# Part of the inverse roots and of the final sums of a recurrent block with experts moves to other engines, with new call orders

## What is computed

```python
xn = _layernorm(x)
s = attn_ref(xn)       # layer norm, k, v, r from mixes of a token and the one before it,
                       # running exp-weighted sums over time (wkv), output product, + xn;
                       # then layer norm, square(relu(xk @ f_kw)) @ f_vw, times sigmoid(xr @ f_rw), + x
shared_out = _swiglu(xn, shared_gate, shared_up, shared_down)
top_id = argmax(xn @ gate_w.T); score = sigmoid(max(xn @ gate_w.T))
routed_out = sum over e of _swiglu(where(top_id == e, xn * score, 0), w_gate[e], w_up[e], w_down[e])
out = x + s * silu(shared_out + routed_out)
```

## Time and profile before

| | |
|---|---|
| time, median of 3 runs | 515.05 us (514.98 to 516.02) |
| time of the profiled execution | 514.26 us |
| span of its instructions | 512.5 us |
| PE busy | 453.8 us (89%) |
| DVE busy | 394.2 us (77%) |
| ACT busy | 338.9 us (66%) |
| POOL busy | 327.3 us (64%) |

### The profile page before, as it was taken

How to read it: one execution, slowest core, us unless ns; L and a number is a source line. 1 busy time by engine, 2 the same in 40 slices (tenths; PEclk the granted TensorE clock), 3 DMA queues, 4 the chain that set the end, 5 groups by cost and what they waited for, 6 DMA issues and landing times. The chain is left out here.

```text
span 512.5 us, 9573 instructions
## 1 busy us (share of the span) xinstructions
PE 453.8 (89%) x2689; PEld 339.8 (66%) x2689; DVE 394.2 (77%) x896; ACT 338.9 (66%) x661; POOL 327.3 (64%) x347
## 2 busy tenths in 40 slices
PE   0879897869499898999899989998999998999995
PEld 0656665537257686978697969786978564555663
DVE  4698987889386879688959895889588999677362
ACT  2687766535185769676968686769686859395634
POOL 6437888788785368878787868678857544434010
PEclk9978899969889999999999989999999999999998
DMA  8213641111621045655555546555644346874200
GB/s 249 83 51 91 227 146 42 44 37 60 191 74 44 17 135 165 191 162 161 167 177 159 164 139 195 160 162 165 178 149 139 104 59 110 140 103 63 42 22 20
DMA packets 55060, 61.33 MB, mean 120 GB/s; under 512 B 5904, under 2 KB 43153, under 8 KB 54944
## 3 DMA queue, kind: packets, MB, share of 16 engines
q1 hardware_dynamic: 42672, 47.11, 31.6%
q0 software_dynamic: 11184, 11.94, 10.9%
q10 hardware_dynamic: 1152, 1.67, 1.0%
HBM read 46.97 MB, written 17.59 MB: 126 GB/s over the span
## 5 line engine op out<-in xcount | busy, mean ns | idle before, releaser
L1624 POOL DMA_INDIRECT routed_out<-xh,xs x71 | 77.4, 1090 | 44.1 <-ACT xh L1042 26.9
L475 PEld LDWEIGHTS bank_ring<-xh,ew 128*128 128x128 f32 x568 | 73.0, 194 | 19.2 <-issue 18.5
L1612 POOL DMA_INDIRECT tokens_by_expert<-xn,pos x64 | 71.4, 1116 | 19.5 <-issue 19.5
L475 PE MATMUL bank_ring<-xh,ew 128*128 128x128 f32 x568 | 75.8, 277 | 0.0
L419 PEld LDWEIGHTS bank_out<-fvw,kk 128*128 128x128 f32 x512 | 63.4, 192 | 12.3 <-issue 8.5
L419 PE MATMUL bank_out<-fvw,kk 128*128 128x128 f32 x512 | 66.4, 275 | 0.0
L1619 POOL TENSOR_SCALAR xs<-xs 128x128 f32<-128x128 f32 x71 | 57.2, 809 | 7.7 <-DMA xs<-tokens_by_expert 5.8
L1032 ACT ACTIVATE px<-bank_ring 128x256 f32<-128x256 f32 x71 | 27.2, 383 | 38.1 <-PE bank_ring L475 37.5
L2170 DVE TENSOR_TENSOR hx<-px,bank_ring 128x256 f32<-128x256 f32 x71 | 29.1, 409 | 25.4 <-ACT px L1032 19.2
L984 ACT ACTIVATE z<-x,x_sm 128x128 f32<-128x128 f32 x64 | 26.3, 482 | 27.8 <-POOL x_sm L1597 27.6
L489 PE MATMUL bank_ring<-ew,hx 128*128 128x128 f32 x284 | 43.4, 275 | 0.2 <-issue 0.2
(11 more groups left out here) (177 smaller groups left out, 1106.8 us busy)
## 6 DMA issues: line engine op xcount, KB each, us to landing
ew<-ex_w SPq DMA_DIRECT2D x71, 384.0 KB
xi<-x SPq DMA_DIRECT2D x19, 256.0 KB, 3.7
xs<-tokens_by_expert SPq DMA_DIRECT2D x71, 66.0 KB, 2.7
ew<-routed_out SPq DMA_DIRECT2D x16, 256.0 KB, 3.1
out<-x SPq DMA_DIRECT2D x2, 1664.0 KB
out<-xn POOLq DMA_DIRECT2D x13, 256.0 KB, 4.8
routed_out<-xh,xs POOLq DMA_INDIRECT x71, 2.8
tokens_by_expert<-xn,pos POOLq DMA_INDIRECT x64
```

Of the source, the lines that this page charges most:

```text
L475: last = nc.tensor.matmul(part(GU[n % 2], q, P), part(w, q, P), xt[:, 0:P], start=True, stop=True)
L1612: nc.gpsimd.indirect_dma_start(xs_dram, bass.IndirectOffsetOnAxis(ap=POS[:, t:t + 1], axis=0), XN[:, t * XROW:(t + 1) * XROW], None).then_ ...
L1624: nc.gpsimd.indirect_dma_start(routed_dram, bass.IndirectOffsetOnAxis(ap=XS[(n - 2) % NXS][:, CH:CH + 1].bitcast(i32), axis=0), XH[n % NXH ...
```

## The change

Five things change. **Roots:** `first(c)` takes 4 columns. DVE makes the second layer norm's variance in three parts (chunk 0, chunks 1 to 3, chunks 4 to 15: `second_variance`), whose inverse roots come from POOL for chunk 0 and from ACT's Ln and Exp for the others (`second_rstd`). Of `rstd_of_x2` only the power stays on POOL; DVE does the additions around it (`make_x2`, `bias_of_x2`). **Moved tiles:** `make_d1` and `make_rw` of chunks 0 to 3 go from POOL to DVE. **Final sums:** those of chunks 0 to 10 become one addition each on DVE, in place in the shared result. **Weights:** ACT issues the load of the shared expert's upper weights before the attention's, and four semaphores take the place of one. **Call orders:** every engine's list except SP's is written in another order; 64 scatters count on 8 semaphores where they had 16. The core of the diff:

```diff
+R2_PARTS = (0, 1, 4, CHUNKS)
+ON_VECTOR = (0, 1, 2, 3, 4, 5, 6, 7, 8, 9, 10)
...
+        def summed(p):
+            before = sum(1 for m in SUMS[:p] if m in ON_VECTOR)
+            return (s_fd, before + 1) if SUMS[p] in ON_VECTOR else (s_fy, p - before + 1)
 
...
             logits(0)
             first_transpose(1)
-            pe.wait_ge(s_wa, 16 * 5)
-            shared_part(0, 0)
+            shared_part(0, 1)
             logits(1)
             first_transpose(2)
...
-                                (ATT[:, :], att_w, s_wa), (SUP[:, :], sh_up, s_wa), (SDN[:, :], sh_dn, s_wa),
-                                (FKW[:, :], f_kw, s_wa), (FVW[:, :], f_vw, s_wa)):
+                                (SUP[:, :], sh_up, s_wu), (ATT[:, :], att_w, s_wa), (SDN[:, :], sh_dn, s_wd),
+                                (FKW[:, :], f_kw, s_wf), (FVW[:, :], f_vw, s_wf)):
                 act.dma_start(dst, src).then_inc(s, 16)
...
@@ -939,8 +935,15 @@
                 act.wait_ge(s_rt, g * PLACE + 1)
                 nc.scalar.activation(part(SC, g, GT), part(MX, g, GT), ACT.Tanh, scale=0.5).then_inc(s_th, 1)
 
+            def second_rstd(k):
+                a, b = R2_PARTS[k] * TPC, R2_PARTS[k + 1] * TPC
+                act.wait_ge(s_v2, 3 * k + 3)
+                nc.scalar.activation(R2[:, a:b], V2[:, a:b], ACT.Ln).then_inc(s_r2, 1)
+                act.wait_ge(s_r2, 2 * k + 1)
+                nc.scalar.activation(R2[:, a:b], R2[:, a:b], ACT.Exp, scale=-0.5).then_inc(s_r2, 1)
+
             def halve_output_weights():
-                act.wait_ge(s_wa, 16 * 5)
+                act.wait_ge(s_wa, 16)
                 nc.scalar.activation(part(ATT, 3, CH), part(ATT, 3, CH), ACT.Copy, scale=0.5).then_inc(s_half, 1)
 
...
             def final_part(m):
-                act.wait_ge(s_fy, SUMS.index(m) + 1)
-                nc.scalar.activation(part(XT, m, CHUNK), RING[2][:, :], ACT.Silu).then_inc(s_fw, 1)
+                act.wait_ge(*summed(SUMS.index(m)))
+                y = part(XT, m, CHUNK) if m in ON_VECTOR else RING[2][:, :]
+                nc.scalar.activation(part(XT, m, CHUNK), y, ACT.Silu).then_inc(s_fw, 1)
 
             nc.scalar.preload_act_table_set("natural_log_exp_and_others")
...
             def first(c):
-                a, b = 2 * c * TPC, 2 * (c + 1) * TPC
-                pool.wait_ge(s_ve, 2 * (c + 1))
-                nc.gpsimd.tensor_tensor(RS[:, a:b], VE[:, a:b], NH[:, 0:2 * TPC], ALU.pow).then_inc(s_rs, 1)
+                pool.wait_ge(s_ve, c + 1)
+                nc.gpsimd.tensor_tensor(part(RS, c, TPC), part(VE, c, TPC), NH[:, 0:TPC], ALU.pow).then_inc(s_rs, 1)
 
             def make_d1(c):
                 pool.wait_ge(s_h1, c + 1)
@@ -1582,20 +1589,14 @@
                     pool.wait_ge(s_mix, 3 * c)
                 nc.gpsimd.tensor_tensor(batches(D1[:, :]), now(H1), before(H1), ALU.subtract).then_inc(s_d1, 1)
 
+            def second_rstd_of_first():
+                b = R2_PARTS[1] * TPC
+                pool.wait_ge(s_v2, 3)
+                nc.gpsimd.tensor_tensor(R2[:, 0:b], V2[:, 0:b], NH[:, 0:b], ALU.pow).then_inc(s_r2, 2)
+
             def rstd_of_x2(c):
-                mean, var = stats(MV2, 0, TPC)
-                pool.wait_ge(s_mv2, TPC * (c + 1))
-                if c > 0:
-                    pool.wait_ge(s_z2, TPC * c)
-                settle(pool)
-                nc.gpsimd.tensor_scalar(SM2[:, 0:TPC], var, EPS, None, ALU.add).then_inc(s_sm2, 1)
-                nc.gpsimd.tensor_scalar(SM2[:, 2 * TPC:3 * TPC], mean, -1.0, None, ALU.mult).then_inc(s_nm2, 1)
                 pool.wait_ge(s_sm2, c + 1)
                 nc.gpsimd.tensor_tensor(SM2[:, TPC:2 * TPC], SM2[:, 0:TPC], NH[:, 0:TPC], ALU.pow).then_inc(s_rs2, 1)
-                pool.wait_ge(s_nm2, c + 1)
-                pool.wait_ge(s_rs2, c + 1)
-                nc.gpsimd.tensor_tensor(SM2[:, 2 * TPC:3 * TPC], SM2[:, 2 * TPC:3 * TPC], SM2[:, TPC:2 * TPC],
-                                        ALU.mult).then_inc(s_nb2, 1)
...
-                a = 2 * c * TPC
                 dve.wait_ge(s_mv, TPC * c + TPC)
-                nc.vector.tensor_scalar(VE[:, a:a + TPC], var, EPS, None, ALU.add).then_inc(s_ve, 1)
-                nc.vector.tensor_scalar(VE[:, a + TPC:a + 2 * TPC], var, 1.0 + EPS, EPS * EPS, ALU.mult, ALU.add)\
-                  .then_inc(s_ve, 1)
+                nc.vector.tensor_scalar(part(VE, c, TPC), var, EPS, None, ALU.add).then_inc(s_ve, 1)
 
             def first_bias(c):
-                a, b, t = c * TPC, (c + 1) * TPC, 2 * c * TPC
+                a, b = c * TPC, (c + 1) * TPC
                 mean, var = stats(MV, a, b)
                 dve.wait_ge(s_rs, c + 1)
-                nc.vector.scalar_tensor_tensor(NB[:, a:b], mean, -1.0, RS[:, t:t + TPC], ALU.mult, ALU.mult)\
+                nc.vector.scalar_tensor_tensor(NB[:, a:b], mean, -1.0, RS[:, a:b], ALU.mult, ALU.mult)\
                   .then_inc(s_nb, 1)
-                nc.vector.tensor_tensor(R2[:, a:b], VE[:, t:t + TPC], RS[:, t:t + TPC], ALU.mult).then_inc(s_v2, 1)
-                dve.wait_ge(s_v2, c + 1)
-                nc.vector.tensor_tensor(R2[:, a:b], R2[:, a:b], RS[:, t + TPC:t + 2 * TPC], ALU.mult).then_inc(s_r2, 1)
+
+            def second_variance(k):
+                a, b = R2_PARTS[k] * TPC, R2_PARTS[k + 1] * TPC
+                mean, var = stats(MV, a, b)
+                dve.wait_ge(s_mv, R2_PARTS[k + 1] * TPC)
+                dve.wait_ge(s_rs, R2_PARTS[k + 1])
+                nc.vector.tensor_tensor(V2[:, a:b], var, RS[:, a:b], ALU.mult).then_inc(s_v2, 1)
+                dve.wait_ge(s_v2, 3 * k + 1)
+                nc.vector.tensor_tensor(V2[:, a:b], V2[:, a:b], RS[:, a:b], ALU.mult).then_inc(s_v2, 1)
+                dve.wait_ge(s_v2, 3 * k + 2)
+                nc.vector.tensor_scalar(V2[:, a:b], V2[:, a:b], EPS, None, ALU.add).then_inc(s_v2, 1)
...
                     nc.vector.bn_aggr(part(MV2, j, 2), part(BS2, j, 6)).then_inc(s_mv2, 1)
+                mean, var = stats(MV2, 0, TPC)
+                dve.wait_ge(s_mv2, TPC * c + TPC)
+                nc.vector.tensor_scalar(SM2[:, 0:TPC], var, EPS, None, ALU.add).then_inc(s_sm2, 1)
+
+            def bias_of_x2(c):
+                mean, var = stats(MV2, 0, TPC)
+                dve.wait_ge(s_rs2, c + 1)
+                nc.vector.scalar_tensor_tensor(SM2[:, 2 * TPC:3 * TPC], mean, -1.0, SM2[:, TPC:2 * TPC],
+                                               ALU.mult, ALU.mult).then_inc(s_nb2, 1)
+
+            def make_d1(c):
+                dve.wait_ge(s_h1, c + 1)
+                if c > 0:
+                    dve.wait_ge(s_mix, 3 * c)
+                nc.vector.tensor_tensor(batches(D1[:, :]), now(H1), before(H1), ALU.subtract).then_inc(s_d1, 1)
+
+            def make_rw(c):
+                dve.wait_ge(s_tn, c + 1)
+                dve.wait_ge(s_iq, c + 1)
+                if c > 0:
+                    dve.wait_ge(s_att, c)
+                nc.vector.tensor_tensor(RW[:, :], NUM, LQ[:, :], ALU.mult).then_inc(s_rw, 1)
 
...
+
+            def final_sum(m):
+                p = SUMS.index(m)
+                dve.wait_ge(s_fr_in[p % 4], 16 * (p // 4 + 1))
+                dve.wait_ge(s_sh, m + 1)
+                nc.vector.tensor_tensor(part(XT, m, CHUNK), part(XT, m, CHUNK), RR[p % 4], ALU.add).then_inc(s_fd, 1)
 
```

More of the change, by code:

```diff
@@ L585, in _ @@
+            shared_part(9, 0)
+            key(3)
+            value(3)
+            shared_part(9, 1)
             ffn_receptance(0)
+            pe.wait_ge(s_wf, 16 * 2)
             ffn_key(0, 0)
@@ L828, in _ @@
-            z2_transpose(11)
-            expert_slot(71)
-            value(13)
-            expert_slot(72)
-            late_part(11, 0)
+            ffn_key(10, 1)
+            expert_slot(56)
+            ffn_key(10, 2)
+            ffn_key(10, 3)
+            expert_slot(57)
+            attention_out(11)
+            ffn_value(10, 0)
+            expert_slot(58)
+            receptance(13)
+            expert_slot(59)
+            key(13)
+            ffn_value(10, 1)
+            expert_slot(60)
```

1755 lines of the change are left out of this document (884 added, 871 removed).

## The result

The changed kernel takes 479.6 us (median of 4 runs, 476.0 to 483.3) where the kernel before took 515.2 in the same comparison: a ratio of 0.928, 95% interval 0.923 to 0.934. The profiled run, 483.25 us, is the slowest of the four, 1.5% above the fastest, and the ratio is of the three others (476.0 to 479.9). Measured again beside the first experiments it took 478.5 us (6 runs, 477.9 to 480.8), ratio 0.930 [0.927, 0.933]. The forecast was 491, range 478 to 506.

A forecast was written before the change was run, and what follows sets the result against it. TensorE's list was taken as the bound behind slot 0, with waits deciding the front. Front 160, slots 245.9, tail 78.3 and the last 5.8 gave a span of 490.0 us, plus 1.76 makes 491.8, stated as 491, range 478 to 506.

The forecast's parts named there:

- Final sums: Tail: 22 products of 0.86 us, 18.9 us, leave TensorE; VectorE gets 7.6 us; about 14 us gained after the new wait.
- The shift into the slots: One more chunk's work before slot 72: 15.5 us longer in the slots, 15.6 shorter in the tail, neutral at unchanged fill.
- The new wait of 6 us at chunk 13: Tail: TensorE stands 6 us at chunk 13's receptance for VectorE's mixes, bounds 0 and 10; tail 78.3 us.
- Front, 9 us: Before slot 0: GpSimd loses 13.5 us, last scatter at 143, slot 0 at 160, 9 us earlier; bounds 152 and 169.
- Slots, 245.9: Slot stretch: 227.5 us of TensorE work at fill 0.925, VectorE 83% busy; bounds 240.7 and 252.8.
- Weights and ScalarE's roots, 0: Shared weights' load with four semaphores, and ScalarE's extra table loads and activations in the front: 0 us.
- (1): Rival: VectorE sets the slots' pace, 255 us, time 501; chance 0.22 together with (2) and the rule's case.
- (3): Rival: slower than before, VectorE's recurrence late by every slot; 526 us at a period of 28; chance 0.04.
- (5): Rival: the final sums don't leave the path, VectorE being full in the tail; 503 to 510 us; chance 0.04.
- (2): Rival: the front gives nothing, slot 0 stays at 169, time 501; chance 0.22 together with (1) and the rule's case.
- (4): Rival: more than forecast, no new TensorE waits and slot 0 at 152; 473 us; chance 0.08.
- The rule of the exclusive lock: Front: eight tiles moved to VectorE each block GpSimd 0.69 us, 5.5 in all; 497 us if scatters are the path.

The follow-up runs named there:

- experiment 1: The kernel before, old call orders kept, with only the final sums of chunks 0 to 10 as VectorE additions: 518.5 us, ratio 1.008.
- experiment 7: The kernel before, old call orders kept, with only the final sums of chunks 6 to 10 on VectorE: 514.0 us, ratio 1.000.
- experiment 2: The changed kernel with the final sums of chunks 0 to 10 back on TensorE: 491.2 us, ratio 0.954 to the kernel before.
- experiment 8: The changed kernel with final sums, moved tiles and roots all undone, leaving new orders and weights' loads: 514.7 us, measured again 507.8.
- experiment 5: The changed kernel with chunk 13's second half of the roots and its mixes earlier on VectorE, ScalarE's steps likewise: 481.1 us, ratio 0.935.
- experiment 9: The changed kernel with VectorE's final sums, all but the first, put off behind chunk 13's mixes and chunk 11's shared products, ScalarE's list likewise: 518.5 us.
- experiment 6: The kernel before, old call orders kept, with differences and products of chunks 0 to 3 on VectorE: 524.0 us; with products placed later 534.3.

## Why the prediction was right, and where it was not

The time lies in the stated range, near its lower end: 35.5 us were gained where 24 were forecast. Most of the difference is the front.

- **What bounds the kernel: right behind slot 0, with a gap.** TensorE's fill in the slots came out at 227.5/243.8 = 0.933 (forecast 0.925) and in the tail at 66.9/77.5 = 0.863 with the new wait. "Whatever leaves it there counts almost whole" holds in the new orders only. In the old ones TensorE looked full (103.4 of 108.3) and yet nothing came of 18.9 or of 8.6 us less (experiments 1 and 7): its work just filled a time that the recurrence set.
- **Final sums, -18.9 us of TensorE work and 14 us of gain: right in sum.** Undoing them costs 12.7 (experiment 2).
- **The shift into the slots, "neutral": wrong.** The orders alone bring 20.9 in the tail for 14.5 in the slots, 6 us. The step priced the shift by TensorE's work alone (14.4 us both ways) and left out what it does to the recurrence: chunk 15's denominator starts 12.9 us behind slot 72 in experiment 8 and 62.4 before, the tail no longer waits for it, and its fill rises to 0.98 (66.9 and the 18.9 of the sums, over 87.4). In the sum the error was offset: the sums bring 10.9 us in the tail where the forecast had 14.4 (18.9/0.925 less 6). That the tail came out within 0.8 us is in part luck.
- **"VectorE has room in the tail": true of the whole, false of the place.** It is at 68% there, and between 400 and 425 us at 96% in the first profile and 99% in the second. That is where the new wait comes from.
- **The new wait of 6 us at chunk 13: right in size, in part in place.** 5.1 us of standing, of which only 2.0 are at the receptance where all 6 had been put; the mixes' product starts 19.1 us behind slot 72's end, where +19.5 had been worked out. The lower clock behind it, some 3 us, was not foreseen. Work at full-clock prices, all stands of the tail and the lower clock (66.9, 6.6 and 3.1) make 76.6 of the 77.5 us; the forecast got there with a fill of 0.925 instead. What the step put down to the order of the calls looks more like VectorE's load (experiments 5 and 9).
- **Front, 9 us: the mis-sized term; 14.8 measured in the first profile, 17.3 in the second.** GpSimd's relief of 13.5 and the last scatter at 143 were right (142.9). The step that failed is the choice of 160 between 152 and 169, on the reason that TensorE had been late by itself in the last 8 us. The runs show that with the new orders slot 0 follows the last scatter: with 7.1 us of tiles or 6 us of roots back on GpSimd it moves by 8.4 and 8.9 us. Of TensorE's own lateness only the 0.8 us are left by which slot 0 came nearer to the scatters.
- **Slots, 245.9: right** (243.8). The chain of VectorE did not set the pace, though it was busy for 218.5 of 243.8 us, 90%; forecast were 83%. That sum has a slip, 1.3 fewer slot products a chunk where 71/9 less 71/10 is 0.8, which is only 0.3 us; measured are 21.8 us of VectorE a chunk for the 20.5 forecast.
- **Weights and ScalarE's roots, 0: not tried alone.** They are within the 6 us of the orders.
- **The rivals.** (1), (3) and (5) did not come; (5) names what does happen in the old orders (experiment 1). (2), the front giving nothing, is what the tiles do when they are moved alone (experiment 6). (4) is nearest in the front, 154.1 and 151.6 for its 152, while its tail without a wait did not come.
- **The rule of the exclusive lock**, as a loss of 5.5 us in the front: did not come; the tiles on VectorE bring 7.4 us, and the scatters' median is 0.96 us with the tiles there and 0.99 with them on GpSimd. The collision itself is there on both sides: GpSimd's remaining differences take 1.03 us at best and 2.01 at worst; VectorE's four moved ones take 0.67 to 0.69, but one of its sixteen of the second layer norm took 2.29 where 0.68 is usual, with a whole difference of GpSimd (227.74 to 228.79 us) inside its time. The longest of them in the kernel before took 0.70.

```profile
L2152 DVE TENSOR_TENSOR d<-h x16: 665/684/2293, 119.1 to 464.7; 128x512 f32<-128x512 f32 x16
...
227.06 2.29 DVE L2152 TENSOR_TENSOR d<-h 128x512 f32<-128x512 f32 x1
...
227.74 1.05 POOL L1590 TENSOR_TENSOR d<-h 128x512 f32<-128x512 f32 x1
```

  The Trainium skill, SBUF — State Buffer, section "SBUF: two separate sides", says that of two such operations the second waits for the whole of the first; the trace agrees, by 1.0 us for GpSimd and 1.6 us for VectorE. How often the two met in the front was not counted.
